# Five-layer transformer kernel on one core: setup reordered, keys and queries stored term by term, early keys and causal maxima moved

## The chip, the cores and the metric

The kernel runs on one core of a Trainium2 chip. The metric is the device time of one launch in microseconds (us). The engines are TensorE (PE, matmuls; PEld its weight loads), VectorE (DVE), ScalarE (ACT), GpSimd (POOL) and SyncE (SP). SP computes nothing here: it issues most DMAs. POOL issues weight loads.

## The reference, cut to what matters

Batch 1, 1024 tokens (x) of width 128, a context of 6404 tokens, 16 heads of width 8, everything in float32. There are four attentions. The first (cross0) attends from x to the context with a mask that drops up to a quarter of the context at its end; the second (self0) is plain self-attention; the third (self1) is causal; the fourth (cross1) attends to the same context without a mask. Each is followed by projections, layer norms or a feed-forward block.

```python
def _mha(q_in, k_in, v_in, Wq, Wk, Wv, bv, causal):
    q = jnp.einsum('bsd,hde->bhse', q_in, Wq)
    k = jnp.einsum('btd,hde->bhte', k_in, Wk)
    v = jnp.einsum('btd,hde->bhte', v_in, Wv) + bv[None, :, None, :]
    scores = jnp.einsum('bhse,bhte->bhst', q, k) * scale
    ...
    attn = jax.nn.softmax(scores, axis=-1)
    return jnp.einsum('bhst,bhte->bhse', attn, v)
...
x = x + _L0_xattn_ref(_layernorm(x), ctx_1024, mask, ...)   # cross0, masked
x = x + _L0_ffn_ref(_layernorm(x), ...)                     # self0, top-2 of 8 experts
x = x + _L1_xattn_ref(_layernorm(x), ctx_1024, ...)         # self1 causal, cross1, ffn
x = x + _L1_ffn_ref(_layernorm(x), ...)                     # top-2 of 8 experts, shared expert
```

## The kernel before, in words

**Precision by terms.** Scores must be accurate in float32, but the score matmuls run in bfloat16. So a projected key or query value is split into three bfloat16 parts (`split`): part 1 is the rounded value, the rest after it gives part 2, the rest after that part 3. A score is the sum of six products of parts, and the six stand below each other in the contraction: a head of width 8 takes 6 x 8 = 48 rows of a stage tile. `Q_PARTS` and `K_PARTS` (L38, L39) say which part stands in which of the six terms. Three further rows hold minus the query's maximum, also in three parts, and in cross0 one more row holds the mask.

**The split** works in jobs of 512 columns: PE projects into PSUM, ACT rounds to part 1 (L937), DVE subtracts (`take_rest`, L1104), ACT rounds to part 2 (L942), POOL subtracts to part 3 (L753), and SP stores the parts to DRAM (`store_parts`, L503): one DMA for the three parts of a key job (L511), six for a query job (L515), one for each term. There are four buffers of parts (`SPLITS`). cross0 has 13 key jobs and 2 query jobs, self0 and self1 two of each, cross1 has 2 query jobs. In cross0, before the split, DVE multiplies each projected key by `keep`, which is 1 or 0 by the mask (`make_keep`, L1173), from a mask that was loaded to all 128 partitions.

**Setup of cross0.** x is normalised and turned first, then the context is turned tile by tile (`turn_context`, L1835), projected and split. After the last key job SP writes the mask row and the row of ones into the four slots of both sides (`load_mask_row`, L491: 24 DMAs), then stores the query jobs.

**Staging.** A head is staged from DRAM into one of four slots of `k_stages` and `q_stages`, on two sides of 64 partitions: in a cross attention each side holds half of the keys (`stage_keys`, L522: three DMAs per side, of 24, 16 and 8 rows) and the same queries (`stage_queries`, L534); in a self attention each side is a head of a pair (`stage`, L594: the same three, and one for the queries).

**Main loops.** A cross attention makes 32 passes (16 heads, two halves of the queries). In each, 28 units of scores on PE (`pass_a`, L1677) go to DVE, which takes their maxima (L1234); maxima are joined, split by POOL (`split_maxima`), turned by PE, copied by ACT (`copy_turned`) and put into the query stage by SP (`put_maxima`, L546); then the scores are made again with the maximum subtracted (`pass_b`, L1719), ACT takes the exponential (L1028), and PE multiplies by the values. `pass_a` runs 40 units ahead (`a.ahead`). Between the first 28 units PE also projects the values of the context, 13 banks, which ACT copies out (L952). The 13 key jobs of cross1 (`early_jobs`) are done inside cross0, one in each of 13 of its second 16 passes, as one more item among the units (L1680 to L1690): DVE copies it (`take_key`), POOL alone splits it (`split_early`, L838).

**Self attentions** make 16 passes (8 pairs, two halves). `exps`, `evacuate` (ACT copies the sums out of PSUM in step 2 of the next pass, L969) and `store_out` (SP stores them, L616, and the next `evacuate` waits for that) follow the same pattern. The order on SP within a pass j is written out at L638 to L650:

```python
                for j in range(a.n):
                    pair, half = a.passes[j]
                    if half == 0 and pair >= 1 and pair + a.ring - 1 < H // 2:
                        sp.wait_ge(sem(a.name + "_scores"),
                                   pair_tile_use(a, j - 1, len(a.steps[j - 1]) - 1, a.sides - 1) + 1)
                        stage(pair + a.ring - 1)
                    if j + 1 < a.n:
                        put_maxima(j + 1)
                    if 1 <= j < a.n - 1:
                        store_out(j - 1)
```

In self1 the turn of the maxima of pass j + 1 comes in step 0 of pass j where j is even (`turn_step`), elsewhere in step 3. All order between engines is by semaphores, written by hand.

## Time and profile before

| | |
|---|---|
| median of 3 runs | 2730.98 us (2729.42 to 2733.01) |
| the profiled execution: its own time, its span | 2728.58 us, 2726.7 us |
| TensorE clock granted, mean over the span | 0.941 of full speed |
| busy: PE, DVE, ACT, POOL | 87%, 86%, 78%, 10% |
| cross0, until its first pass of exponentials runs | 0 to 141.7 us |
| cross0, main loop | 141.7 us to about 1114 us |
| self0 and its experts | to about 1394 us |
| self1 | to about 1590 us |
| cross1 and what follows | to the end |

The busy shares are means over stages with different limits. The chain of waits tells, at each moment, which work the end of the kernel hangs on; the timeline of a stretch tells what lies beside it.

### The profile page before, as it was taken

The page shows a single profiled execution, that of the slowest core. Times are in us where ns is not written, and L with a number is a line of the kernel's source. Part 1 is how long each engine was busy: PE and PEld are TensorE (multiplying, and loading weights), DVE is VectorE, ACT ScalarE, POOL GpSimd, SP SyncE. Part 2 cuts the span into 40 slices and gives each one's busy share as a digit, 9 for nine tenths or more (in the row PEclk, how much of TensorE's full clock was granted, in tenths as well). Part 3 has the DMA queues.
Part 4 walks back from the last instruction along what each step waited for, and adds up shares of the span by engine and source line. Part 5 has one row for each costly group of instructions (what it writes and reads, how often), then busy time and mean ns, then how long its engine had stood idle before and what let it go on. Part 6 is the DMA issues. An engine that isn't in the chain of part 4 may idle for free.

```text
span 2726.7 us, 59202 instructions
## 1 busy us (share of the span) xinstructions
PE 2384.8 (87%) x23163; PEld 751.8 (28%) x23163; DVE 2352.2 (86%) x2668; ACT 2134.0 (78%) x4065; POOL 274.8 (10%) x740
## 2 busy tenths in 40 slices
PE   4499999999999999489758848999999999999986
PEld 2222222222222222122322213222222222222224
DVE  6699999999999997499636649999999999999945
ACT  3189999999889899469615625999999999999971
POOL 5000110012111110100001100000000100000000
PEclk8799999999999999789878968999999999999998
DMA  4201111111111110111121030111111111111000
GB/s 144 73 24 41 41 35 45 43 44 41 47 49 41 41 43 7 46 50 33 36 61 41 30 99 4 38 34 30 30 40 33 30 30 41 31 30 32 17 3 8
DMA packets 75513, 107.98 MB, mean 40 GB/s; under 512 B 17061, under 2 KB 55849, under 8 KB 75241
## 3 DMA queue, kind: packets, MB, share of 16 engines
q1 hardware_dynamic: 73128, 99.79, 12.4%
q0 software_dynamic: 2112, 4.42, 0.9%
q8 instruction: 189, 3.10, 0.5%
q14 instruction: 84, 0.68, 0.1%
HBM read 73.45 MB, written 21.90 MB: 35 GB/s over the span
## 4 chain that ended last, share of the span: by engine, by line
PE 68%; DVE 18%; ACT 5%; SPq 3%; issue 3%; DMA 2%; POOL 0%; ACTq 0%; DVEq 0%
PE ps L1498 68%; DVE maxima L1234 12%; ACT probs L1028 4%; SPq L515 1%; DVE maxima L1193 1%; SPq L600 1%; ACT probs L986 1%; DVE scratch L1104 1%; DMA o_self<-acc_out 0%; PE ps L1504 0%; DVE stats L1110 0%; DMA scratch<-o_self 0%; DMA q_stages<-max_rows 0%; DVE z L1104 0%; DMA q_stages<-q_cross 0%
## 5 line engine op out<-in xcount | busy, mean ns | idle before, releaser
L1234 DVE TENSOR_REDUCE maxima<-ps 128x1 f32<-128x920 f32 x1792 | 1887.8, 1111 | 96.4 <-PE ps L1498 96.3
L1028 ACT ACTIVATE probs<-ps 128x512 f32<-128x512 f32 (+1 forms) x3264 | 1761.3, 594 | 159.9 <-PE ps L1498 159.7
L1498 PE MATMUL ps<-probs,v_stage 128*16 128x256 f32 x14208 | 1159.5, 393 | 0.6 <-ACT acc_out L1017 0.4
L1498 PE MATMUL ps<-k_stages,q_stages 64*128 64x460 bf16 (+2 forms) x4032 | 756.3, 373 | 187.3 <-DMA q_stages<-q_cross 64.4
L1498 PE MATMUL ps<-q_stages,k_stages 64*128 64x512 bf16 (+1 forms) x3712 | 725.8, 381 | 45.1 <-ACT probs L986 16.9
L1498 PEld LDWEIGHTS ps<-k_stages,q_stages 64*128 64x128 bf16 x4032 | 193.6, 93 | 1049.7 <-issue 494.3
L1498 PEld LDWEIGHTS ps<-probs,v_stage 128*16 128x16 f32 x14208 | 236.9, 94 | 412.2 <-issue 362.9
L1193 DVE TENSOR_REDUCE maxima<-ps 128x2 f32<-128x1024 f32 (+1 forms) x224 | 240.1, 1108 | 94.5 <-PE ps L1498 90.9
L986 ACT ACTIVATE probs<-ps 128x512 f32<-128x512 f32 x448 | 224.2, 554 | 72.7 <-PE ps L1498 71.7
L1498 PEld LDWEIGHTS ps<-q_stages,k_stages 64*128 64x128 bf16 x3712 | 187.4, 93 | 277.4 <-ACT probs L1028 69.4
L952 ACT ACTIVATE by_key<-ps 128x512 f32<-128x512 f32 (+1 forms) x30 | 17.5, 583 | 146.2 <-PE ps L1498 146.2
L759 POOL COPY v_stage<-by_key 128x400 f32<-128x400 f32 x64 | 33.1, 517 | 901.1 <-PE ps L1498 785.8
L811 POOL CAST half_parts<-neg_max 128x4 bf16<-128x4 f32 x64 | 11.9, 187 | 851.4 <-DVE neg_max L1253 794.5
L1104 DVE TENSOR_TENSOR scratch<-scratch 112x512 f32<-112x512 f32 (+1 forms) x14 | 13.6, 982 | 66.0 <-DMA scratch<-acc_out 39.7
L904 ACT ACTIVATE std<-var_eps 128x4 f32<-128x4 f32 x18 | 3.7, 205 | 70.9 <-DVE var_eps L1116 70.9
L1104 DVE TENSOR_TENSOR probs<-ps,probs 128x512 f32<-128x512 f32 x36 | 24.5, 689 | 19.8 <-ACT probs L1088 8.2
L1017 ACT ACTIVATE acc_out<-ps 128x512 f32<-128x512 f32 x64 | 38.2, 597 | 0.3 <-PE ps L1498 0.3
L1504 PE MATMUL ps<-ident,z 128*128 128x128 f32 x32 | 8.1, 403 | 32.0 <-DVE z L1126 18.5
L1504 PE MATMUL ps<-ident,xn 128*128 128x128 f32 x24 | 6.6, 430 | 31.5 <-DVE xn L1104 18.0
L783 POOL CAST max_parts<-neg_max 128x8 bf16<-128x8 f32 x32 | 6.1, 189 | 208.5 <-DVE neg_max L1204 162.4
L753 POOL TENSOR_TENSOR probs<-probs 128x512 bf16<-128x512 f32 x10 | 11.2, 1151 | 149.8 <-ACT probs L942 149.8
L1104 DVE TENSOR_TENSOR z<-ps,z 128x512 f32<-128x512 f32 (+2 forms) x10 | 6.7, 674 | 21.0 <-PE ps L1498 14.6
(233 smaller groups left out, 965.4 us busy)
## 6 DMA issues: line engine op xcount, KB each, us to landing
q_stages<-q_cross SPq DMA_DIRECT2D x256, 48.0 KB, 2.6
k_stages<-k_cross SPq DMA_DIRECT2D x64, 150.2 KB
k_stages<-k_cross SPq DMA_DIRECT2D x64, 150.0 KB
scratch<-acc_out SPq DMA_DIRECT2D x496, 16.0 KB
k_stages<-k_cross SPq DMA_DIRECT2D x64, 100.1 KB
k_stages<-k_cross SPq DMA_DIRECT2D x64, 100.0 KB
q_stages<-q_self SPq DMA_DIRECT2D x32, 192.0 KB
k_cross<-probs SPq DMA_DIRECT2D x12, 384.0 KB, 2.8
```

Of the source, the lines that this page charges most:

```text
L515: sp.dma_start(a.q_dram[:, term * E:(term + 1) * E, c0:c0 + n], src[:, part, 0:n]).then_inc(done, DMA)
L600: sp.dma_start(k_stage(a, slot)[base + row:base + row + parts_ * E, :], a.k_dram[0:parts_, h * E:(h + 1) * E, :]).then_inc(done, DMA)
L759: nc.gpsimd.tensor_copy(v_stage[:, par, 0:full, 0:E], src[:, 0:full, :]).then_inc(sem(a.name + "_v_staged"), 1)
L952: last = nc.scalar.activation(by_key[:, t:t + full, :], src[:, 0:full, :], ACT.Copy)
L986: return nc.scalar.activation(probs[:, i % a.p_slots, low:BANK], ps[:, b_bank(a, use), low:BANK], ACT.Exp, scale=float(E) ** -0.5)
L1017: nc.scalar.activation(acc_out[:], ps[:, ACC_BANK, :], ACT.Copy).then_inc(sem(a.name + "_acc_copied"), 1)
L1028: return nc.scalar.activation(probs[0:m, probs_slot(a, j, i), :], ps[0:m, b_bank(a, use), :], ACT.Exp, scale=float(E) ** -0.5)
L1104: return nc.vector.tensor_tensor(out_, a, b, op)
L1193: nc.vector.tensor_reduce(pair_maxima[:, j % 2, :, qt % QT, c // BANK], ps[:, A_BANK + 2 * (g % 2):A_BANK + 2 * (g % 2) + 2, 0:n], AX_X, A ...
L1234: nc.vector.tensor_reduce(maxima[:, at, seg:seg + 1], ps[:, A_BANK + 2 * (k % 2):A_BANK + 2 * (k % 2) + 2, 0:a.segment], AX_XY, ALU.max).t ...
L1498: return nc.tensor.matmul(out_, lhsT, rhs, start=start, stop=stop)
L1504: last = nc.tensor.transpose(ps[:, bank, t * P:(t + 1) * P], src[:, b * QT + t, :], ident[:])
```

## The change

1. **Setup order.** SP loads the weights and the first context tiles before x; the turning of x is moved from ahead of the context into jobs 4 and 6 (`SETUP_TURNS`). The constants that are not needed at once are made on POOL later, after the first maxima (`later_constants`).
2. **Mask.** Keys are no longer multiplied by `keep`; the mask row alone drops them. The mask is loaded to one partition. The row of ones is written early by 2 DMAs, the mask row by 2, where there were 24.
3. **Terms in DRAM.** DRAM now holds six terms of keys and of queries. A job of either kind is stored by three DMAs of 3, 2 and 1 terms (`store_job`), so a key job moves 768 KB where it moved 384 KB. Staging takes one DMA per side for keys and one for each query stage. The last job of each attention is stored from ACT's queue.
4. **Staging of self attentions** begins when all but the last query job is stored; pair 0 gets its first half of queries then and the remainder afterwards (`stage_rest`, awaited by `q_rest`).
5. **Early keys** of cross1 move out of the 13 passes to the first 28 units of cross0, where PE now has a value bank or an early key job after nearly every unit (`a.fill`). Here ACT copies and rounds, POOL makes both subtractions, SP stores; before its first exponential ACT waits until all are stored.
6. **Causal maxima.** In self1, on SP, `put_maxima(j + 1)` goes ahead of `stage` where `turn_step[j]` is 0.

```diff
-            sp.dma_start(x[:], x_dram).then_inc(sem("x_in"), DMA)
...
+                if t == 0:
+                    sp.dma_start(x[:], x_dram).then_inc(sem("x_in"), DMA)
...
+        def store_job(queue, a, i):
+            kind, c0, n = a.jobs[i]
+            src, done = a.parts[:, i % SPLITS, :, 0:n], stored(a, i)
+            queue.wait_ge(sem("split_part3"), a.jobs_before + i + 1)
+            first = 0
+            for part, terms in enumerate((3, 2, 1)):
+                if kind == "k":
+                    dst, part_ = a.k_dram, src[:, 0:terms]
+                else:
+                    dst, part_ = a.q_dram, src[:, part:part + 1].to_broadcast([P, terms, n])
+                queue.dma_start(dst[first:first + terms, :, c0:c0 + n].rearrange("a p c -> p a c"),
+                                part_).then_inc(done, DMA)
+                first += terms
...
-                    for row, parts_ in ((0, 3), (3 * E, 2), (5 * E, 1)):
-                        sp.dma_start(dst[base + row:base + row + parts_ * E, 0:count],
-                                     a.k_dram[0:parts_, h * E:(h + 1) * E, first:first + count]).then_inc(done, DMA)
+                    sp.dma_start(dst[base:base + ROW_MAX, 0:count],
+                                 a.k_dram[:, h * E:(h + 1) * E, first:first + count]).then_inc(done, DMA)
...
-                put_maxima(0)
+                if a is cross0:
+                    for i in range(len(early.jobs)):
+                        if i == len(early.jobs) - 2:
+                            put_maxima(0)
+                        store_job(sp, early, i)
+                else:
+                    put_maxima(0)
...
                 for j in range(a.n):
                     pair, half = a.passes[j]
+                    if a.turn_step[j] == 0 and j + 1 < a.n:
+                        put_maxima(j + 1)
                     if half == 0 and pair >= 1 and pair + a.ring - 1 < H // 2:
...
-                    if j + 1 < a.n:
+                    if a.turn_step[j] != 0 and j + 1 < a.n:
                         put_maxima(j + 1)
...
+                if a is cross0:
+                    wait_stored(act, early, len(early.jobs) - SPLITS, len(early.jobs))
...
-                        tt(a.whole[:, i % SPLITS, 0:n], ps[:, a.job_banks[i], 0:n], keep[:, c0:c0 + n],
-                           ALU.mult).then_inc(sem(a.name + "_whole"), 1)
...
-            for b in range(HALVES):
-                turn(b, xn, 1, 6 + b)
-            for b in range(HALVES):
-                half_turned(b, 1)
...
+                if i in SETUP_TURNS:
+                    b = SETUP_TURNS.index(i)
+                    if b == 1:
+                        half_turned(0, 1)
+                    turn(b, xn, 1, 3)
```

The order of the instructions, at three places. **SP, setup of cross0, before**, from the last key job to the first head (`k_cross` and `q_cross` are the DRAM copies, `probs` holds the parts):

```order
L511 DMA k_cross<-probs 128x3x260
L498 DMA k_stages<-k_stages 1x12x267
L501 DMA q_stages<-ones_row 1x16x64 x2
...
L515 DMA q_cross<-probs 16x8x512 x12
L529 DMA k_stages<-k_cross 24x1x3204
L529 DMA k_stages<-k_cross 16x1x3204
L529 DMA k_stages<-k_cross 8x3204
L529 DMA k_stages<-k_cross 24x1x3200
```

The same place now:

```order
L497 DMA k_cross<-probs 128x3x260
L497 DMA k_cross<-probs 128x2x260
L497 DMA k_cross<-probs 128x260
L538 DMA k_stages<-probs 1x4x3204
L538 DMA k_stages<-probs 1x4x3200
L497 DMA q_cross<-probs 128x3x512
L497 DMA q_cross<-probs 128x2x512
L497 DMA q_cross<-probs 128x512
L548 DMA k_stages<-k_cross 48x1x3204
L548 DMA k_stages<-k_cross 48x1x3200
L563 DMA q_stages<-q_cross 48x1x512 x2
```

Between the last key job and the first key DMA of a head there were 36 DMAs and are 5.

**PE, the first units of cross0, before** (460-column matmuls are two to a unit, 128-column ones are a value bank):

```order
L1498 MATMUL ps<-xT,w_q_cross 128x512 x2
L1498 MATMUL ps<-k_stages,q_stages 128x460 x6
L1498 MATMUL ps<-w_kv_cross,ctxT 128x128 x4
L1498 MATMUL ps<-k_stages,q_stages 128x460 x4
L1498 MATMUL ps<-w_kv_cross,ctxT 128x128 x4
L1498 MATMUL ps<-k_stages,q_stages 128x460 x4
```

Now (`w_k_cross` are early key jobs):

```order
L1559 MATMUL ps<-xT,w_q_cross 128x512 x2
L1559 MATMUL ps<-k_stages,q_stages 128x460 x4
L1559 MATMUL ps<-ctxT,w_k_cross 128x512
L1559 MATMUL ps<-k_stages,q_stages 128x460 x2
L1559 MATMUL ps<-w_kv_cross,ctxT 128x128 x4
L1559 MATMUL ps<-k_stages,q_stages 128x460 x2
L1559 MATMUL ps<-ctxT,w_k_cross 128x512
L1559 MATMUL ps<-k_stages,q_stages 128x460 x2
```

There is now a job between any two units, an early key job and a value bank by turns.

**SP, pass 2 of self1 now** (the first pass with staging; the passes 4, 6 and 8 read alike):

```order
L646 DMA q_stages<-max_rows 3x4x128 [waits self1_max_rows]
L646 DMA q_stages<-max_rows 3x4x128
L618 DMA k_stages<-k_self 48x1x1024 [waits self1_scores]
L626 DMA q_stages<-q_self 48x1x1024 x2
L618 DMA k_stages<-k_self 48x1x1024
L626 DMA q_stages<-q_self 48x1x1024 x2
L658 DMA o_self<-acc_out 2x8x512 [waits self1_acc_copied]
L658 DMA o_self<-acc_out 2x8x512 x3
```

Before, the two rows of maxima stood between the staging and the stores of `acc_out`, and the staging had 8 DMAs where it has 6.

## Rows read from the trace of the kernel before

**Rows 1.** The page: PE busy by fortieths, and the chain of waits by engine

```profile
PE   4499999999999999489758848999999999999986
...
PE 68%; DVE 18%; ACT 5%; SPq 3%; issue 3%; DMA 2%; POOL 0%; ACTq 0%; DVEq 0%
```

**Rows 2.** Windows of the setup (window, PE, PEld, DVE, ACT, POOL, clock, DMA share, GB/s)

```profile
60.00:80.00 20.00, 0.00 (x0) 0.00 (x0) 0.00 (x0) 0.00 (x0) 0.00 (x0) 0.50 0.29 76
...
100.00:120.00 20.00, 16.70 (x114) 10.65 (x113) 19.93 (x21) 5.79 (x10) 0.00 (x0) 1.00 0.20 69
```

**Rows 3.** Timeline of the setup (start, us, engine, line, operation; idle before it)

```profile
13.37 1.13 DVE L1126 TENSOR_SCALAR xn<-x,mean_var,rstd 128x128 f32<-128x128 f32 x4
...
21.83 0.63 ACT L937 ACTIVATE probs<-scratch 128x512 bf16<-128x512 f32 x1 [1.84 <-DVE scratch L1104]
...
29.27 26.49 SPq L511 DMA_DIRECT2D k_cross<-probs  x13
...
71.57 7.70 SPq L515 DMA_DIRECT2D q_cross<-probs  x12
81.21 3.88 SPq L529 DMA_DIRECT2D k_stages<-k_cross  x6
...
93.45 0.95 PE L1498 MATMUL ps<-k_stages,q_stages 64*128 64x460 bf16 x4 [41.45 <-DMA q_stages<-q_cross]
```

**Rows 4.** DMA view, 29 to 42 us, in 40 slices

```profile
GB/s 0 0 0 98 353 347 350 63 195 353 340 312 10 25 0 0 296 350 343 221 0 0 0 50 347 350 343 120 0 0 0 148 350 347 334 32 0 0 0 249
```

**Rows 5.** Timeline and chain of the first units of cross0

```profile
37.56 1.13 PE L1498 MATMUL ps<-ctxT,w_kv_cross 128*128 128x512 f32 x2 [0.94 <-ACT ctxT L917]
...
52.07 3.30 POOL L753 TENSOR_TENSOR probs<-scratch,probs 128x512 bf16<-128x512 f32 x3 [1.28 <-ACT probs L942]
...
112.25 1.16 PE L1498 MATMUL ps<-w_kv_cross,ctxT 128*128 128x128 f32 x8
```

**Rows 6.** Chain of waits over the whole span (start, us, what)

```profile
125.28 16.38 DVE maxima L1234 x16
...
595.81 17.82 PE ps L1498 x195
...
625.92 18.88 PE ps L1498 x197
...
1030.58 17.82 PE ps L1498 x195
```

**Rows 7.** Timeline around the staging of self0

```profile
1140.16 0.39 SPq L511 DMA_DIRECT2D k_self<-probs  x1
...
1151.78 1.94 SPq L600 DMA_DIRECT2D k_stages<-k_self  x3
...
1159.26 0.61 PE L1498 MATMUL ps<-k_stages,q_stages 64*128 64x512 bf16 x2 [19.58 <-DMA q_stages<-q_self]
```

**Rows 8.** Timeline of pass 2 of self1, and PE's waits from 1440 to 1584 us

```profile
1458.29 1.87 SPq L600 DMA_DIRECT2D k_stages<-k_self  x3
...
1460.50 0.26 ACT L966 ACTIVATE max_rows<-ps 24x128 bf16<-24x128 bf16 x1
...
1464.40 2.50 SPq L624 DMA_DIRECT2D o_self<-acc_out  x4
...
1466.06 0.39 PE L1498 MATMUL ps<-q_stages,k_stages 64*128 64x512 bf16 x2 [1.51 <-DMA q_stages<-max_rows]
...
1468.94 0.60 ACT L976 ACTIVATE acc_out<-ps 128x512 f32<-128x512 f32 x1
...
PE ps L1498 <- DMA q_stages<-max_rows: 8.9, 5, 2.2
```

**Rows 9.** Timeline around the staging of cross1, and the DMA rate from 1610 us

```profile
1610.33 13.11 SPq L515 DMA_DIRECT2D q_cross<-probs  x12
...
1630.86 0.95 PE L1498 MATMUL ps<-k_stages,q_stages 64*128 64x460 bf16 x4 [22.94 <-DMA q_stages<-q_cross]
...
GB/s 51 51 51 203 205 221 260 227 215 174 64 51 51 51 51 80 240 64 64 195 137 51 107 225 139 219 250 233 207 162 47 47 47 49 47 35 8 0 0 98
```

More of the change, by code:

```diff
@@ L235, in transformer @@
         SIDE = P // 2
-        ROWS_IN = cross0.sides * cross0.ring * 3
+        ROWS_IN = cross0.sides * 2
         QT = NT // HALVES
@@ L447, in moe1_banks, with q_rest_count @@
             return (5, 6, 7) if u % 2 == 0 else (0, 1, 2)
+        def q_rest_count(a):
+            return (1 + (a is self1)) * 2 * a.sides * DMA
         def b_bank(a, use):
@@ L459, in max_goal, with wait_stored @@
             return min(a.n * n, a.ahead + j * n + t + 1 + sum(t >= at for at in a.more_at))
+        JOB_DMAS = 3
         def stored(a, i):
+            if a is not early and i == len(a.jobs) - 1:
+                return sem("q1_stored")
             return sem(a.name + f"_stored{i % SPLITS}" if a.masked else a.name + "_stored")
         def stored_count(a, i):
-            jobs = range(i % SPLITS, i + 1, SPLITS) if a.masked else range(len(a.jobs))
-            return DMA * sum(TERMS if a.jobs[j][0] == "q" else 1 for j in jobs)
+            if a is not early and i == len(a.jobs) - 1:
+                return (attentions.index(a) + 1) * JOB_DMAS * DMA
+            return (i // SPLITS + 1 if a.masked else len(a.jobs) - 1) * JOB_DMAS * DMA
+        def wait_stored(queue, a, first, last):
+            for i in range(first, last):
+                queue.wait_ge(stored(a, i), stored_count(a, i))
+        def store_job(queue, a, i):
[11 more added lines that the diff above has]
+                first += terms
         RESULTS = ["cross0", "self0", "moe0", "self1", "cross1", "ffn", "moe1"]
@@ L671, in _ @@
                     sp.wait_ge(sem("self1_scores"), 2 * len(self1.all_steps) + self1.n)
-                    sp.wait_ge(sem("early_stored"), cross1.n_k_jobs * DMA)
+                    wait_stored(sp, early, len(early.jobs) - SPLITS, len(early.jobs))
                     for j in range(cross1.ring):
@@ L732, in _ @@
-            for late in (late_out["self0"], late_out["self1"]):
-                for g in range(4):
-                    col = late[:, g // 2, :] if late.shape[2] == VCOLS else late[:, g // 2, D:D + 1]
-                    first = 32 * g + (0 if late.shape[2] == VCOLS else E)
-                    link(nc.gpsimd.affine_select(out=col, in_=col, compare_op=ALU.not_equal, fill=1.0, base=-first,
-                                                 pattern=[[-1, col.shape[1]]], channel_multiplier=1))
             nc.gpsimd.memset(ones_row[:], 1.0)
@@ L958, in short_attention, with fill @@
+            def fill(a):
+                for kind, i in itertools.chain(*a.fill):
+                    if kind == "values":
+                        take_values(a, i)
+                    else:
+                        take_early(i)
+                if a is cross0:
+                    early_part2(len(early.jobs) - 1)
             def short_attention(a):
```

425 lines of the change are left out of this document (226 added, 199 removed).

## The prediction

> **What bounds the kernel now.** I read the page first. PE is the last link of the chain for 68% of the span, and the fortieths show it at nine tenths in two long stretches, the main loops of the cross attentions [rows 1]. The change hardly touches these; it works on the low digits between them. So I read the chain of waits over the whole span for where the loops begin and how long a pass takes, and the timeline of each gap for who releases whom.
>
> In the setup no engine computes from 60 to 80 us [rows 2]. The parts of the 13 key jobs are stored by 55.8 us (29.27 + 26.49); the query stores begin at 71.57 us. Between lie 24 small DMAs of mask and ones, 15.8 us in which SP alone is the limit. Then the query stores, their landing, the first staging at 81.21 us, and PE's first unit at 93.45 us, after 41.45 us idle [rows 3]. The main loop follows after 28 units (125.28 us) and 16 more units on DVE, at 141.7 us [rows 6]. A pass takes 30.1 us, but the 13 passes with an early key take 404.66 us together (625.92 to 1030.58), 31.13 each [rows 6]. The gaps at self0, self1 and cross1 look alike: PE idle for 19.6 and 22.9 us until a query stage lands [rows 7, 9]. In self1 PE waited 8.9 us for maxima, in five waits [rows 8].
>
> **The change part by part.** The sum is against the profiled execution, 2728.58 us.
>
> *First unit of cross0, from 93.45 to about 55.5 us: -38.* (a) Part 1 of job 0 was made at 21.83 us, behind the turning of x and the mask product [rows 3]. Now the context is turned while DVE normalises; DVE is free at 14.5 us (13.37 + 1.13), so I put part 1 at 15 us and the first store, which came 7.4 us behind part 1 and has less before it now (a subtraction and the product are gone), 4 us behind: 19 us. (b) Jobs came every 2.2 us in the mean, 12 periods from 29.27 to about 55.4 us. Now ACT has three copies of about 0.6 us per job, 1.8 us. But a key job stores 768 KB, and the store rate stands at 350 GB/s while a job is being written [rows 4]: 2.2 us. I take 2.2; 1.8, and 2.6 if DMA keeps only 300 GB/s, are the ends. 12.5 jobs and 2 us to land give 48.5 us (43 to 52). (c) The key DMAs of head 0 go then, 1.5 us of issue, but its queries wait for query job 0, which shares the DMA engines with job 1 on ACT's queue: 3 us more; then two query DMAs and their landing, some 4 us. That is 7 us from the first key DMA to the first unit; as now it would be 12.2 us (81.21 to 93.45) [rows 3], the upper end; with one third of the key DMAs 3.5 us is the lower. I take 7, nearer the lower, because the 12.2 is a queue: from 1625 us, while the last of it drains, the DMA moves 47 to 49 GB/s where 350 are possible, so few engines carry them [rows 4, 9], and six terms in one DMA should spread better than 3, 2 and 1. The Trainium skill (DMA: Bandwidth & Descriptors, "Why a DMA increments its semaphore by 16 and not by 1") says a DMA runs on the largest number of engines up to 16 that divides the outermost sizes of both its sides: 3 and 2 for the old key DMAs, 16 for the old query DMAs, 6 for both now. The tail of 50 GB/s agrees with that; by it the first unit would come about 5 us after the first key DMA and the sum would be 2 us lower. Loading x third instead of first costs nothing: DVE clears `k_stages` until 8.5 us anyway. The early weight is one DMA beside an 800 KB mask load that is gone. The constants made later on POOL cost nothing: about 15 us of POOL after the first maxima, while the next are needed 24 us on.
>
> *The first 28 units: +10.* They took 31.8 us (93.45 to 125.28), set by DVE at 1.02 us a unit behind a cold start. Now PE has 28 units of 0.27 us (0.95 us for two of them at half clock [rows 3], a little over half of that each at full), 13 value banks of 1.16 and 13 early jobs of 1.1 [rows 5]: 37 us at full clock. Part 3 on POOL takes 1.1 us [rows 5], two subtractions a job 2.3 us, and ACT's four copies about 2.3 us; both are below the 2.8 us that PE needs for a pair, so PE sets the pace. Before, the clock was full from 100 us, 7 us after PE began [rows 2]; in those 7 us an item takes twice as long, which costs 3 us: 40 us, +8. The first turn of maxima stands 4 units behind the 28th, and POOL reaches it only after the last early job, 7 to 8 us behind its projection: about 1.5 us late. ACT's wait for the last early stores (two puts of maxima, six stores, landing: 8 us behind the first maxima) ends when the first scores are ready, and so costs nothing; if stores run late it costs their lateness. Lower end +4 (DVE's pace with PE just behind), upper +28 (half clock throughout).
>
> *Main loop of cross0: -13.2*, that is 13 x 30.11 - 404.66 [rows 6].
>
> *self0: -2.5.* Staging began 11.6 us after the first store and the first unit came 7.5 us after that (1151.78 to 1159.26) [rows 7]. The stores are no faster: four jobs of 768 KB are 3.07 MB, 8.8 us at 350 GB/s [rows 4] and 2 to land, against 11.6. Pair 0 now needs four DMAs instead of eight, with half of the queries: 5 us. Ends 0 and -6. The remainder is needed a pass later and SP's total is 26 DMAs instead of 32, each dearer (below), so put_maxima(0) stays where it is.
>
> *self1: +6.5.* Its first unit gains the same 2.5 us, but SP's staging, not the unit, holds the first maxima, so 1 us is left. Then the four passes with staging. Before, maxima ready at 1460.76 waited for the staging (from 1458.29) and PE resumed at 1466.06. Now they go at once: PE could resume near 1464. But the staging, and behind it `store_out`, now stand behind that put. Ready 1460.76, the put 1.5, staging S, the stores 2.5 (1464.40 on) and 1.7 to land: 1466.5 + S. ACT's `evacuate` of this pass, which was at 1468.94, waits for that [rows 8]. S was 4.5 us for eight DMAs. A DMA whose two sides differ in shape, as the new six all do, took 0.6 to 0.7 us (1.87 us for the three key DMAs of a side) [rows 8], so S is about 4.3 and `evacuate` comes 1.9 us later: 4 x 1.9 = +7.5, less 1. If they cost 0.36 us like a plain store, S is 2.2 and nothing is lost; if the wait for maxima simply goes, -7. Ends -8 and +9.
>
> *cross1: -11.* Before, 12 query stores began at 1610.33 and PE at 1630.86, 20.5 us on, with 13.1 us of issue [rows 9]. Now query job 0 is three DMAs of SP's and job 1 three of ACT's: 1.54 MB, 4.4 us, 2 to land; then the query DMAs of head 0, 1.5 us and 2 to land: 9.5 us. Its keys are staged from 1587 us with 8 DMAs for 24 and are in before. Ends -9 and -13.
>
> Sum: -38 + 10 - 13.2 - 2.5 + 6.5 - 11 = -48. 2728.58 - 48 = 2680.6; the median of the runs is 2.4 us above the profiled execution, so **2683 us**. A measurement of this kernel tells 0.2%, 5.5 us, from no change.
>
> **The rivals.** *A, self1's waits vanish.* For it: 8.9 us of waits for maxima, four of the five in staging passes [rows 8]. Against: the stores' landing had no slack. If the six DMAs are cheap, self1 is -8 instead of +6.5: 2668 us. Chance 0.22.
>
> *B, the first units stay slow.* PE at half clock, or ACT waiting for early stores. For it: 0.50 of the clock stood from 60 to 80 us, and the early stores add 9.6 MB while three heads are staged. Against: PE has no idle there, and 9.6 MB is 28 us at 350 GB/s [rows 2, 4]. It takes back 15 to 25 us: 2703 us. Chance 0.12.
>
> *C, slower than before: a stage DMA of six terms runs on one engine.* If the tail's 50 GB/s are two engines, one moves 25 [rows 9]. A head is 792 KB of keys and queries; on one engine 31.7 us, above the 30.1 us of a pass [rows 6]. Both main loops would then be set by DMA: +1.6 x 62 passes = 99, the first unit +27, cross1's queries behind four heads of keys +60: 2683 + 186 = 2869 us. It decides once less than 792 KB / 30.1 us = 26 GB/s are reached. Against it: the tail alone still moves 47 to 49. Chance 0.03. The rule of the Trainium skill named above says six engines, so it speaks against C.
>
> *D, the early setup does not come off*: the jobs take 2.6 us and staging its 12.2 us; the first unit is at about 66 us: 2693 us. The chance, 0.08, is inside the range.
>
> **How the numbers follow.** The forecast has 0.55, A 0.22, B 0.12, D 0.08, C 0.03. The range takes A, D and most of B: 2662 to 2703 us. Faster by over 0.2% in all but C and an unknown mishap: 0.95; same 0.02; slower 0.03.
>
> **What the profile would show.** First unit of cross0 at 53 to 58 us; DMA near full from 19 to 46 us, and jobs every 2.2 us; 28 units in 38 to 43 us with PE over nine tenths; no pass of 31.1 us. self0 and self1: the first unit some 5 us behind the first staging DMA. In self1 SP's put of the maxima before the staging, ACT's `evacuate` behind a DMA, passes with staging 20 to 21 us a pair instead of 18.5 to 19.7. cross1: first unit 9 to 10 us behind the first store. Wrong I am if PE waits in the first units for ACT or the clock stays low there, if pairs in self1 take 17.5 us, or if any head of the main loops waits for its stage.

## The result, and the profile after

The changed kernel takes 2706.76 us (median of 4 runs, 2704.30 to 2708.58), the kernel before 2731.74 us (4 runs beside it). The ratio is 0.9909, with a 95% interval of 0.9892 to 0.9926: faster by 25 us, where the forecast was 48 us and its range ended at 2703. The sign was right and the size about half.

The page of the changed kernel, answering [rows 1]. Of the fortieths (68 us each) the second rose from 4 to 8, since the main loop begins sooner; but the 22nd and 23rd, which are self1, fell from 8 to 7. In the chain DVE fell from 18 to 15% and DMA rose from 2 to 4%.

```profile
PE   4899999999999999499757758999999999999986
...
PE 70%; DVE 15%; ACT 5%; DMA 4%; SPq 3%; issue 3%; POOL 1%; ACTq 0%; DVEq 0%; POOLq 0%
```

The profiled executions have spans of 2726.7 us before and 2702.6 us after, 24.1 us apart. Eight marks in both chains of waits show where the gain arose. Each mark is the start of the same piece of work; the gain so far is after minus before.

| mark | before | after | gain so far | this stage | forecast |
|---|---|---|---|---|---|
| first unit of cross0 | 93.45 | 65.44 | -28.0 | -28.0 | -38 |
| first PE piece of the main loop, behind 44 units | 141.71 | 129.56 | -12.2 | +15.8 | +10 |
| same piece, last pass but one | 1060.68 | 1035.12 | -25.6 | -13.4 | -13.2 |
| first unit of self0 | 1159.26 | 1129.76 | -29.5 | -3.9 | -2.5 |
| self1, PE's piece before the first staging pass | 1452.37 | 1420.46 | -31.9 | -2.4 | self1 in all: |
| self1, the same behind four staging passes | 1528.34 | 1515.16 | -13.2 | +18.7 | +6.5 |
| self1, load of the result | 1578.93 | 1567.56 | -11.4 | +1.8 | |
| main loop of cross1 | 1679.80 | 1655.56 | -24.2 | -12.9 | -11 |

The same rows of the chain of waits after the change (start, us, what), whole span cut at the stages:

```profile
58.02 7.29 DMA q_stages<-q_cross
...
77.34 7.97 DMA k_cross<-probs
...
129.56 1.53 PE ps L1559 x4
```

```profile
1420.46 7.14 PE ps L1559 x75
...
1436.99 4.48 DMA o_self<-acc_out
...
1443.51 8.72 PE ps L1559 x75
...
1461.60 4.18 DMA o_self<-acc_out
...
1515.16 9.98 PE ps L1559 x75
...
1567.56 5.01 DMA scratch<-o_self
```

So three stages missed, and they miss on the same side: the setup by 10 us, the first units by 6, self1 by 12 (18.1 in its three lines against 6.5). The main loop, self0 and cross1 came within 2 us of their terms.

**Setup.** The timeline of the setup, answering [rows 3] (start, us, engine, line, operation; idle before it):

```profile
14.04 0.60 ACT L988 ACTIVATE probs<-ps 128x512 bf16<-128x512 f32 x1 [1.16 <-PE ps L1559]
...
22.29 0.60 ACT L988 ACTIVATE probs<-ps 128x512 bf16<-128x512 f32 x1 [1.88 <-DMA k_cross<-probs]
...
49.61 0.60 ACT L988 ACTIVATE probs<-ps 128x512 bf16<-128x512 f32 x1 [1.82 <-DMA k_cross<-probs]
```

```profile
54.12 2.17 SPq L548 DMA_DIRECT2D k_stages<-k_cross  x2
57.29 1.42 SPq L563 DMA_DIRECT2D q_stages<-q_cross  x2
...
65.44 0.95 PE L1559 MATMUL ps<-k_stages,q_stages 64*128 64x460 bf16 x4 [20.97 <-DMA q_stages<-q_cross]
```

Part 1 of job 0 is made at 14.04 us and that of the fifteenth and last job at 49.61, so the jobs come every 2.54 us in the mean (35.57 / 14), not every 2.2. That mean holds the first four, which fill the four buffers 1.3 to 1.5 us apart. From the fifth on (22.29 us) ACT waits each time for the store of the job four before, and a job takes 2.73 us (27.32 / 10). The DMA engines are full meanwhile. The first key DMA goes at 54.12 us and not at 48.5, and PE's first unit follows 11.3 us later and not 7.

**First units.** Windows (window, PE, PEld, DVE, ACT, POOL, clock, DMA share, GB/s) and ACT's waits up to 130 us (engine, tile, line, releaser: us in total, times, longest), answering [rows 2]:

```profile
20.00:25.00 5.00, 4.15 (x20) 2.33 (x19) 2.95 (x5) 2.19 (x5) 1.84 (x2) 1.00 1.01 339
30.00:35.00 5.00, 1.77 (x7) 0.66 (x5) 3.14 (x5) 3.20 (x6) 1.71 (x2) 0.93 1.11 272
60.00:65.00 5.00, 0.00 (x0) 0.00 (x0) 0.00 (x0) 0.00 (x0) 0.00 (x0) 0.50 0.39 143
75.00:80.00 5.00, 5.00 (x29) 2.80 (x28) 3.98 (x5) 3.97 (x8) 4.05 (x5) 1.00 0.70 248
80.00:85.00 5.00, 2.63 (x14) 1.26 (x13) 3.27 (x3) 0.49 (x2) 1.84 (x2) 1.00 0.96 323
85.00:90.00 5.00, 3.94 (x11) 2.05 (x11) 1.12 (x1) 3.98 (x7) 2.76 (x3) 0.55 0.26 81
```

```profile
ACT probs L988 <- DMA k_cross<-probs: 15.7, 11, 2.3
...
ACT L1113 <- DMA k_cross<-probs: 8.0, 1, 8.0
ACT probs L1026 <- DMA k_cross<-probs: 7.9, 4, 4.9
```

PE is full at the full clock from 75 to 80 us, stops at 82.6 us, and goes on at 86.06 us at a clock of 0.55. ACT waited 4.92 us for the first early store, whose issue (76.38 us, on time) and landing (85.3 us) lie 8 to 9 us apart. Ahead of it in the queue were four heads of staging, four times 792 KB or 3.2 MB, which moved at 143 GB/s with a DMA share of 0.39. At the end ACT waits again, 8.0 us, for the last early stores, ahead of its first exponential.

**self1.** The waits of ACT from 1384 to 1584 us, and SP's timeline of the first staging pass, answering [rows 8]:

```profile
ACT acc_out L1060 <- DMA o_self<-acc_out: 23.3, 6, 6.2
```

```profile
1428.87 1.48 SPq L646 DMA_DIRECT2D q_stages<-max_rows  x2
1430.39 0.78 SPq L618 DMA_DIRECT2D k_stages<-k_self  x1
...
1434.97 2.60 SPq L658 DMA_DIRECT2D o_self<-acc_out  x4
```

```profile
1441.55 0.60 ACT L1060 ACTIVATE acc_out<-ps 128x512 f32<-128x512 f32 x1 [6.23 <-DMA o_self<-acc_out]
```

```profile
1442.69 0.61 PE L1559 MATMUL ps<-q_stages,k_stages 64*128 64x512 bf16 x2 [6.97 <-ACT probs L1070]
```

Before the change ACT's evacuation waited for DMA for 0.7 us in all of self1, now 23.3 us. The maxima go out at 1428.87, the staging from 1430.39 to 1434.97 (4.6 us), the stores behind it, and they land at 1441.5; ACT stands at its evacuation for 6.23 us and PE, which needs ACT's exponentials, for 6.97 us. Each such stop costs more than its own length: the granted clock, 1.00 before it, is 0.50 from 1442.5 to 1447 us, and PE's next piece of 75 matmuls takes 8.72 us (the line at 1443.51 above) where it took 7.14 us ahead of the stop.

### The profile page after: what moved, and what is told of

Its sections match the earlier page's. It is cut to its first block, busy times and chain, and to the rows that moved or that the text cites. A ratio compares the mean times of both kernels' runs of the same rounds, so it can differ in the third digit from the quotient of the medians.

```text
span 2702.6 us, 58908 instructions
## 1 busy us (share of the span) xinstructions
PE 2381.8 (88%) x23163; PEld 749.6 (28%) x23163; DVE 2334.1 (86%) x2629; ACT 2153.9 (80%) x4104; POOL 258.2 (10%) x720
## 4 chain that ended last, share of the span: by engine, by line
PE 70%; DVE 15%; ACT 5%; DMA 4%; SPq 3%; issue 3%; POOL 1%; ACTq 0%; DVEq 0%; POOLq 0%
PE ps L1559 69%; DVE maxima L1311 11%; ACT probs L1113 3%; DMA k_cross<-probs 1%; DMA o_self<-acc_out 1%; ACT probs L1070 1%; SPq L497 1%; SPq L626 1%; DVE maxima L1270 1%; SPq L658 1%; POOL probs L816 1%; SPq L618 0%; DVE stats L1202 0%; PE ps L1565 0%; DMA scratch<-o_self 0%
## 5 line engine op out<-in xcount | busy, mean ns | idle before, releaser
L1196 DVE TENSOR_TENSOR probs<-ps,probs 128x512 f32<-128x512 f32 x36 | 24.5, 688 | 19.7 <-ACT probs L1180 8.2
L1060 ACT ACTIVATE acc_out<-ps 128x512 f32<-128x512 f32 x32 | 19.2, 599 | 25.6 <-DMA o_self<-acc_out 23.3
L1102 ACT ACTIVATE acc_out<-ps 128x512 f32<-128x512 f32 x64 | 38.2, 597 | 0.2 <-PE ps L1559 0.2
L988 ACT ACTIVATE probs<-ps 128x512 bf16<-128x512 f32 (+1 forms) x25 | 14.7, 589 | 28.6 <-DMA k_cross<-probs 15.7
```

The costliest lines, as they stand in the source:

```text
L1102: nc.scalar.activation(acc_out[:], ps[:, ACC_BANK, :], ACT.Copy).then_inc(sem(a.name + "_acc_copied"), 1)
L1196: return nc.vector.tensor_tensor(out_, a, b, op)
```

## The experiments

The two theories I set against each other for what went missing: **backlog** (staging DMAs on few engines, issued ahead of urgent stores on the same queue, delay them), and **own cost** (the stores, the staging form or the landing cost what they cost wherever they stand). The ratios are all to the kernel before, which ran beside each batch: 2731.7 us beside the change, 2731.4 beside e1 to e4, 2729.4 beside f1 to f4 and 2730.3 beside g1 and g2. Differences of medians between batches, as in the last column, carry up to 2 us of that.

| run | median us | ratio, 95% interval | against the change |
|---|---|---|---|
| stores first in self1 (e1) | 2677.52 | 0.9808 (0.9791 to 0.9824) | -29.2 |
| old order in self1 (e2) | 2687.47 | 0.9842 (0.9826 to 0.9859) | -19.3 |
| heads 2 and 3 behind the early stores (e3) | 2704.12 | 0.9896 (0.9880 to 0.9913) | -2.6 |
| keys stored once (e4) | 2726.53 | 0.9979 (0.9970 to 0.9989) | +19.8 |
| e1 and first maxima of self1 early (f1) | 2674.98 | 0.9800 (0.9785 to 0.9815) | -31.8 |
| e1, e3 and maxima behind all early stores (f2) | 2669.61 | 0.9780 (0.9767 to 0.9793) | -37.2 |
| f1 and f2 together (f4) | 2667.96 | 0.9777 (0.9763 to 0.9790) | -38.8 |
| f4, and cross0's keys stored once (f3) | 2665.68 | 0.9765 (0.9752 to 0.9778) | -41.1 |
| rows layout alone (g1) | 2680.85 | 0.9824 (0.9810 to 0.9837) | -25.9 |
| f4 and rows layout (g2) | 2662.75 | 0.9757 (0.9744 to 0.9770) | -44.0 |

**e1: stores ahead of staging in self1.** Only the order of SP's instructions in that attention is changed:

```diff
                     if a.turn_step[j] == 0 and j + 1 < a.n:
                         put_maxima(j + 1)
-                    if half == 0 and pair >= 1 and pair + a.ring - 1 < H // 2:
+                    if not a.causal and half == 0 and pair >= 1 and pair + a.ring - 1 < H // 2:
                         ...
                         stage(pair + a.ring - 1)
                     if a.turn_step[j] != 0 and j + 1 < a.n:
                         put_maxima(j + 1)
                     if 1 <= j < a.n - 1:
                         store_out(j - 1)
+                    if a.causal and half == 0 and pair >= 1 and pair + a.ring - 1 < H // 2:
+                        ...
+                        stage(pair + a.ring - 1)
```

> Changed kernel, but in attention 1 of the second layer (self1) SP issues put of maxima, stores of the output, and only then the six staging DMAs. Theory (the stores stand behind 4.6 us of staging on SP, and then land in 4.5 instead of 2.5 us since the staging is ahead of them in the DMA queues, and ACT's evacuate waits for them): the four pairs of passes with staging take about 18.5 us instead of 24.3, the stores land in about 2.5 us, and the time falls by 20 to 24 us, to 2683-2687. Rival (the new staging DMAs themselves, six on few engines, hold up what PE and ACT need, wherever they stand): the pairs stay above 22 us and the time above 2698.

Measured 29.2 us less, more than the 20 to 24 expected. From the chain of waits of this run and ACT's waits in self1:

```profile
1421.35 7.14 PE ps L1564 x75
...
1433.82 2.50 DMA o_self<-acc_out
1438.29 7.23 PE ps L1564 x75
...
1489.24 7.22 PE ps L1564 x75
```

```profile
ACT acc_out L1065 <- DMA o_self<-acc_out: 1.1, 6, 0.2
```

A pair takes 17.0 us (67.9 for four) instead of 23.7 (94.7 for four), and the stores land in 2.50 us instead of 4.48. Another 2.9 us come in the passes behind (1489.24 to 1538.78, the load of the result, against 1515.16 to 1567.56). The staging DMAs are the same six with the same issue; only what stands behind them is different. The rival of own cost is out for self1. Part of the gain is clock: no stop, and the granted clock stays at 1.00 through the four pairs, so that PE's pieces of about 75 matmuls take 7.14 to 7.23 us where the changed kernel has 8.72, 8.53, 8.57 and, behind the fourth pair, 9.98 us; that is 4.4 us of the 26.8 in the pairs and nearly all of the 2.9 behind them. The kernel before also lost time here, 19.0 us a pair, but to another wait: PE waited 8.9 us in all for maxima that stood behind the staging.

**e2: the old order in self1** (staging, maxima, stores):

```diff
-                    if a.turn_step[j] == 0 and j + 1 < a.n:
-                        put_maxima(j + 1)
                     if half == 0 and pair >= 1 and pair + a.ring - 1 < H // 2:
                         ...
-                    if a.turn_step[j] != 0 and j + 1 < a.n:
+                    if j + 1 < a.n:
                         put_maxima(j + 1)
```

> Changed kernel with the order before in self1: staging, then maxima, then stores. Theory of the order: the pairs with staging take 19 to 20 us again as before the change, the time falls by 16 to 20 us, to 2687-2691. Rival (new form of the staging DMAs): nothing comes back, 2702 or more.

Measured 19.3 us less, as the theory of the order has it. Chain of waits of e2:

```profile
1423.62 5.89 PE ps L1557 x64
...
1500.07 7.14 PE ps L1557 x75
```

Four pairs take 76.4 us, against 76.0 before the change (1452.37 to 1528.34 in the table) and 94.7 in the changed kernel. So the one edit of putting the causal maxima ahead of the staging cost about 19 us by itself; the new form of the staging cost nothing measurable there. Of e1's 29 us, then, 19 undo this edit, and about 10 are gained on the old order.

**e3: heads 2 and 3 of cross0 staged behind the early stores.**

```diff
-                for j in range(a.ring):
+                for j in range(2 if a is cross0 else a.ring):
...
                     for i in range(len(early.jobs)):
                         ...
                         store_job(sp, early, i)
+                    for j in range(2, a.ring):
+                        stage_keys(a, j)
+                        stage_queries(j)
```

> Changed kernel, but in cross0 heads 2 and 3 are staged behind the stores of the early jobs instead of before them. Theory (the first early store waits 8 us for 3.2 MB of staging that moves at only 143 GB/s; PE then stops from 80.5 to 86 us and runs at half clock after it): the first early store lands in about 4 us, PE has no idle of over 2 us in the first 28 units, the main loop begins 7 to 9 us earlier, 2698-2700. Rival (the stores of early keys are limited by their own 786 KB a job): the stop only comes later, and under 3 us are won, 2704-2707.

In the profile the stop is gone. Windows and chain of e3:

```profile
70.00:80.00 10.00, 10.00 (x51) 5.62 (x51) 7.18 (x8) 6.93 (x14) 6.19 (x6) 0.93 0.23 82
80.00:90.00 10.00, 10.00 (x54) 5.27 (x54) 8.40 (x8) 8.21 (x15) 8.58 (x8) 1.00 0.87 297
```

```profile
65.74 20.64 PE ps L1562 x90
...
124.44 19.98 PE ps L1562 x195
```

PE is full from 70 to 90 us at a clock of 0.93 to 1.00, and the main loop begins at 124.44 instead of 129.56 us, 5.1 us sooner; expected were 7 to 9. The time fell by only 2.6 us, with intervals that overlap: by the times alone no gain is shown, and they lie where the rival had put them (2704 to 2707), while the trace shows the stop gone, as the theory had it. The chain of that run says where the gain went in one execution: PE's piece before the staging passes of self1 still is 3.8 us ahead (1416.64 against 1420.46), and behind the four staging passes 0.7 us (1514.47 against 1515.16), since they took 97.8 instead of 94.7 us. But the profiled execution of e3 is one of its slower ones (2706.36 of 2698.94 to 2707.53) and that of the changed kernel its fastest (2704.30), so that e3's own effect on self1 is not shown. In f2, where self1 is mended, the gain reaches the end.

**e4: key parts once in DRAM.** One store of 384 KB a key job of both cross attentions instead of three of 768 KB together; a head's keys staged by three DMAs a side:

```diff
-    a.stage_dmas = a.first_dmas = 2 * a.sides
+    a.stage_dmas = a.first_dmas = 4 * a.sides
...
-                    sp.dma_start(dst[base:base + ROW_MAX, 0:count],
-                                 a.k_dram[:, h * E:(h + 1) * E, first:first + count]).then_inc(done, DMA)
+                    for row, parts_ in ((0, 3), (3 * E, 2), (5 * E, 1)):
+                        sp.dma_start(dst[base + row:base + row + parts_ * E, 0:count],
+                                     a.k_dram[0:parts_, h * E:(h + 1) * E, first:first + count]).then_inc(done, DMA)
```

> Changed kernel, but key parts of both cross attentions lie once in DRAM (three terms, one store of 384 KB a job instead of three of 786 KB together), and a head's keys are staged by three DMAs a side as before the change. Theory (setup and early jobs are bound by the bytes stored, 786 KB at about 300 GB/s): jobs come every 1.9 to 2.1 us instead of 2.6, the last key part is stored 7 us earlier, and the slower staging takes back 3 to 5; first unit at 60 to 63 us instead of 65.4; ACT no longer stops for early stores except for the first; 2698-2703. Rival (jobs are bound by the chain ACT, DVE, ACT, POOL and the landing time of a store, not by bytes): jobs stay at 2.5 us or more, the first unit comes at 68 to 71 us, and the time is 2708 or more.

Slower than the change by 19.8 us. The time lies where the rival had it (2708 or more), but the rival's jobs of 2.5 us or more did not come, and the theory's time is missed by over 23 us. Part 1 of its jobs, its first unit, its windows and the largest pieces of its chain:

```profile
14.07 0.60 ACT L996 ACTIVATE probs<-ps 128x512 bf16<-128x512 f32 x1 [1.19 <-PE ps L1567]
...
40.05 0.60 ACT L996 ACTIVATE probs<-ps 128x512 bf16<-128x512 f32 x1 [0.58 <-DMA k_cross<-probs]
```

```profile
59.92 0.95 PE L1567 MATMUL ps<-k_stages,q_stages 64*128 64x460 bf16 x4 [21.31 <-DMA q_stages<-q_cross]
```

```profile
70.00:80.00 10.00, 6.89 (x40) 3.92 (x38) 6.70 (x6) 4.20 (x8) 5.15 (x5) 0.98 0.20 70
80.00:90.00 10.00, 0.00 (x0) 0.00 (x0) 0.00 (x0) 0.00 (x0) 0.00 (x0) 0.50 0.45 164
```

```profile
80.82 11.96 DMA k_cross<-probs
```

```profile
1609.30 16.23 DMA q_cross<-probs
```

With half of the bytes the jobs come every 1.86 us (14.07 to 40.05), and the first unit 5.5 us sooner. The edit also leaves one store DMA a job where there were three; but in the changed kernel the DMA engines are full and SP is not (39 stores of 0.53 us in 32 us), so it is the bytes stored that bind its setup. But with three DMAs a side the staging moves 70 GB/s at a DMA share of 0.20. SP gets its early stores out only at 80.82 us instead of 76.38, the first land 12 us behind their issue, PE waits 16.6 us from 77 us on, and the main loop begins 6.3 us later (135.89). At cross1 the query stores land in 16.2 us instead of 3.8, and its main loop begins 23.3 us later (1678.82). That is the backlog again, at half the rate. Neither expectation had priced it.

**f1: the first maxima of self1 ahead of the last pair's staging.**

```diff
                 for pair in range(a.ring):
+                    if a.causal and pair == a.ring - 1:
+                        put_maxima(0)
                     stage(pair)
...
-                put_maxima(0)
+                if not a.causal:
+                    put_maxima(0)
```

> The version with stores ahead of staging in self1, and there also the first put of maxima moved from behind all four pairs' staging to ahead of the last pair's. Theory (ACT has the maxima of pass 0 at 1398.7 us, SP gets to them at 1402.7, since it issues 26 staging DMAs of 0.74 us each first): 3 to 4 us less than the stores-first version, 2673-2675. Rival (something else holds pass 0, such as the landing of the staging): nothing, 2677-2678.

Measured 2.5 us less than e1, which ran in another batch, with ranges that overlap. The marks say that the edit itself brought less: from the end of the first key landing to the PE piece of the pass, 35.95 us (1386.92 to 1422.87) against 36.79 (1384.56 to 1421.35). SP's lateness was there, but DVE's maxima stood right behind it in the chain. The expectation of 3 to 4 us was a miss.

**f2: the order in cross0 as in e3, and the first maxima behind all early stores.**

```diff
                     for i in range(len(early.jobs)):
-                        if i == len(early.jobs) - 2:
-                            put_maxima(0)
                         store_job(sp, early, i)
+                    put_maxima(0)
```

> The version with stores ahead of staging in self1, and in cross0 heads 2 and 3 staged behind the early stores, and the first put of maxima behind all early stores instead of ahead of the last two jobs'. Theory (SP holds the last two jobs' stores back until the maxima are there, and ACT waits for their landing before its first exponential; heads 2 and 3 delay the first early store): the loop begins 5 us earlier by the staging as seen before and 3 to 4 more by the last stores, 2668-2671 in all, now that self1 can no longer eat it. Rival (the first scores need the maxima, and their put is what decides): only the 5 us, 2672-2673.

7.9 us less than e1, and the main loop starts at 123.24 instead of 130.27 us. Of these 7.0 us e3 alone had 5.1. The chain of f2 at this place:

```profile
105.59 10.24 DVE maxima L1318 x10
...
117.04 1.28 ACT L1120
...
123.24 16.81 PE ps L1566 x151
```

ACT's wait for the last early stores (8.0 us in the changed kernel, 9.1 in e3) is gone, but only 1.2 us came of it against e3 (123.24 for 124.44), where 3 to 4 were expected: DVE's maxima (16 units more) end only at 115.8 us. Even this is not told from chance: f4, whose code is the same up to here, has 121.79 us. The forecast's "costs nothing" for that wait was nearly right; what it cost is its excess over DVE.

**f3 and f4: the orders together, without and with keys stored once in cross0.** f4 is f1 and f2 together; f3 adds the edit of e4 for cross0 alone.

> The three changes of order together: stores ahead of staging and early first maxima in self1, heads 2 and 3 and the maxima behind the early stores in cross0. The terms stand in different stages and should add: 2677.5 - 3.5 - 5 - 3.5 = 2665 to 2667. If they do not (one eats another's gain, as self1 did), 2670 or more.

> All of these together, and cross0's keys stored once (three terms) and staged by three DMAs a side, cross1's as in the changed kernel. Theory (setup is bound by bytes stored; the price of that form was the staging at 70 GB/s of four heads ahead of the early stores and of cross1): first unit at 60 us instead of 65.4, early stores without the stop of 12 us, 5 us below the same version with six terms: 2661-2663. Rival (two heads staged at 70 GB/s still block the first early stores): PE stops at 80 us for 4 us or more, and the time is that of the other version or above, 2666 or more.

f4 took 2667.96 us, 1 us above what was expected. In f3 the first unit stands at 58.99 us and the main loop at 116.08 instead of 121.79 us; with two heads staged in front nothing blocks the early stores. Its median is 2.3 us below f4, with intervals that overlap, so of the 5.7 us of the mark less than half is shown in the time.

**g1 and g2: the same number of DMAs, with rows at one stride.** The layout in DRAM is [channel, term, key] instead of [term, channel, key]; the 48 rows of a head then lie at one stride, and nothing else is changed in g1:

```diff
-            a.k_dram = dram("k_" + a.name, [TERMS, P, a.keys], BF16)
+            a.k_dram = dram("k_" + a.name, [P * TERMS, a.keys], BF16)
...
-                queue.dma_start(dst[first:first + terms, :, c0:c0 + n].rearrange("a p c -> p a c"),
+                queue.dma_start(dst.rearrange("(p a) c -> p a c", a=TERMS)[:, first:first + terms, c0:c0 + n],
...
-                                 a.k_dram[:, h * E:(h + 1) * E, first:first + count]).then_inc(done, DMA)
+                                 a.k_dram[h * ROW_MAX:(h + 1) * ROW_MAX, first:first + count]).then_inc(done, DMA)
```

> Changed kernel with nothing moved; only the layout of keys and queries in DRAM is [channel, term, key] instead of [term, channel, key], so that a head's 48 rows lie at one stride and the two sides of a staging DMA have the same outermost size, 48. Theory (the changed kernel's staging DMAs run on 6 of 16 engines at about 143 GB/s and cost 0.74 us of issue because their sides differ in shape; what went wrong in fill and self1 is this backlog): issue falls to 0.35-0.4 us, staging runs at 250 GB/s or more, the first unit of cross0 comes 3 to 5 us sooner, PE's stop at 80 us goes (5 to 8 us), the self1 pairs with staging fall from 24.3 to about 19.5 us (18 to 20 us in all), self0 gains 1 to 2; together 28 to 34 us: 2673-2679. Rival (the landing and not the number of engines is what costs, or stores in this layout get slower): under 10 us, 2697 or more.

25.9 us less than the change, a little short of the 28 to 34. SP's timeline of a staging pass of self1, two windows of the staging in cross0, and the chain of g1:

```profile
1438.61 0.41 SPq L618 DMA_DIRECT2D k_stages<-k_self  x1
...
1441.40 2.52 SPq L658 DMA_DIRECT2D o_self<-acc_out  x4
```

```profile
63.00:66.00 3.00, 2.86 (x6) 0.66 (x6) 2.14 (x2) 0.00 (x0) 0.00 (x0) 0.50 1.00 165
66.00:69.00 3.00, 3.00 (x17) 1.56 (x16) 2.18 (x2) 1.84 (x4) 1.16 (x1) 0.95 1.08 206
```

```profile
1408.17 7.14 PE ps L1559 x75
...
1443.34 2.51 DMA o_self<-acc_out
...
1490.61 9.44 PE ps L1559 x73
```

The staging takes 2.8 us of issue instead of 4.6. Its heads in cross0 move at 165 to 206 GB/s with all DMA engines busy, instead of 143 with a share of 0.39; expected were 250 or more. The stores behind it land in 2.51 us, PE no longer stops at 80 us, and the main loop begins 6.7 us sooner (122.85). Another 5.6 us come by the start of self1's staging passes (1408.17 against 1420.46), from the stages between. Four pairs of self1 take 82.4 us, 12.3 less than in the changed kernel and 14.5 more than in e1, since the issue still stands ahead of the stores. The first unit came only 2.3 us sooner (63.14): the stores of query job 0, for which its queries wait, land at 57.50 us as before (57.27), and only the landing of the query DMA behind them is shorter, 5.14 us instead of 7.29.

> That layout together with the three changes of order. Theory: in self1 the order already removes what the backlog cost, so of the layout there remain the first unit of cross0 (3 to 5), self0, self1 and cross1 starts (1 to 2 each): 2668 - 6 to 10 = 2658-2662. Rival (the first unit is bound by the landing of a DMA whatever its engines): 2665 or more.

g2 has the lowest median of the study: 2662.75 us, ratio 0.9757 (0.9744 to 0.9770), 44 us below the changed kernel's; its interval overlaps those of f3 and f4. It is 5.2 us below f4, where 6 to 10 were expected. The marks put this between the main loop of cross0 and self1's staging passes (1285.9 us in g2, 1290.7 in f4); the main loop itself begins only 0.2 us sooner (121.57), and the first unit, at 64.44 us, gave not the 3 to 5 expected but 0.7.

## Why the prediction was wrong

**Setup, step (b), mis-sized: -28 instead of -38.** The mechanism was named rightly, a job's 768 KB set its pace, and the upper end of 2.6 us with 300 GB/s kept was in the text. I took 350 GB/s from [rows 4], a rate read while one 384 KB job was written at a time with gaps between. With stores back to back the windows show 339 GB/s of all traffic from 20 us, but 272 from 30 us, and once the buffers are full a job takes 2.73 us, which is 288 GB/s of stores (786 KB in decimal units), below even the 300 of the upper end. With the first four jobs the mean is 2.54 us; over the 12.5 periods of the sum that is 4.3 of the 5.6 us by which the first key DMA was late. The start was 1 us early (18.03 us for 19), and what is left, some 2 us, lies behind the last job: 4.5 us from its part 1 to the first key DMA, which SP issues behind the stores of query job 0. e4 shows the cause: half of the bytes, 1.86 us a job. At the first unit rival D came true, 65.4 us where it said about 66; the forecast of the whole had given it 0.08.

**Setup, step (c), mis-sized.** Between the first key DMA and the first unit lay 11.3 us, nearly the 12.2 of the kernel before, not 7. The 3 us until the queries may go were right (54.12 to 57.27 us, when the stores of query job 0 have landed); the "two query DMAs and their landing, some 4 us" took 8.2, of which the landing is 7.29. I argued that six terms spread better than 3, 2 and 1. They do: 143 GB/s, against 70 in e4. The share of 0.39 is six of sixteen DMA engines, and 143 GB/s is 24 for each, as the 47 to 49 of [rows 9] were for two. The Trainium skill (DMA: Bandwidth & Descriptors, "Why a DMA increments its semaphore by 16 and not by 1") says that such a DMA runs on 6 engines, the largest number up to 16 that divides both outer sizes; the trace agrees, and in g1, where the rule gives 16 for an outer size of 48, the share rose to 1.08. By the rule alone I had put the first unit 5 us behind the first key DMA, and that was wrong: it gives the number of engines, not what else stands in their queues. At 143 GB/s the keys of head 0, 600 KB, take 4.2 us, and the two query DMAs go out 3.2 us behind them. That accounts for a part of the 7.29 us only: from 57.0 to 65.4 us 1.22 MB moved, where keys and queries of head 0 are 0.70 MB together. 0.23 MB of it went over ACT's queue, on which query job 1 was being stored. No run puts the query DMAs ahead of the keys or takes job 1 away, so how the 7.29 us divide stays open.

**The first 28 units: +15.8 instead of +10.** "ACT's wait for early stores costs nothing; if stores run late it costs their lateness." They ran late, by 4.92 us at the first and less at three later ones, and behind PE's stop the granted clock was 0.50 from 86 to 92 us. This is rival B, at a third of its price. What I had not done is to add up what stands in the queue ahead of the first early store: four heads, 3.2 MB, issued from 54 to 74 us, at 143 GB/s 22 us. The prediction compared the 9.6 MB of early stores with 350 GB/s, but the staging cannot use that rate. e3 took out two heads and got 5.1 us back: from its first unit to its main loop it is 58.7 us (65.74 to 124.44), 10.4 more than before the change, where the forecast had +10. So the backlog accounts for this miss to within 1 us.

**self1: +18.1 instead of +6.5.** The formula had the right parts: SP's order is maxima, staging, stores, and ACT's evacuation waits for the landing. S was put at 4.3 us and is 4.6, four times 0.3. The landing was put at 1.7 us behind the last of the four issues, which is 2.3 us counted as the profile counts it, from the start of that issue; in e1 with nothing ahead it is 2.50, but behind six staging DMAs 4.48, 4.18, 3.90 and 3.22 us in the four passes, 6.6 us more than forecast in all. And the stops have a price that the formula left at nothing: PE at a granted clock of 0.50 behind each, 4.4 us over the pieces at 1443.51, 1467.82 and 1491.94 us. 7.5 + 1.2 + 6.6 + 4.4 is 19.7, and 18.7 were measured. So the terms that failed are "1.7 to land" and the clock behind the wait. Rival A, that the waits vanish, went the wrong way, and it had the largest chance of the rivals; the waits for maxima did shrink, from 8.9 to 1.5 us, but into a larger wait of ACT.

**Right:** the main loop of cross0 (-13.4 for -13.2), self0 (-3.9 for -2.5), cross1 (-12.9 for -11, first store 1598.16 us, PE 1606.35 us, 8.2 us where I had said 9.5). Rival C, one engine, did not happen. The range failed because its upper end took in one late stage (B), and here three were late together: the first units and self1 by the same backlog of staging, the setup by the rate of its stores. I had treated their errors as independent.

What stays open: how the 7.29 us of the first query landing divide between the keys ahead, the stores of query job 1 and what was issued behind, since no run changes them one by one, e4 and g1 moving several at once; and whether e3's staging passes of 97.8 us are chance or a result of its own order.

## What to carry to other kernels

Ahead of an order of DMA issues ask, for each store or put that an engine waits for, how many bytes stand before it in the same queue and at what rate these can move, and price its landing from that, not from a landing seen with an empty queue. Put what someone waits for first, and prefetches last: this cost nothing in code and was worth more (29 us, of which 19 undo one edit of the change) than the whole change. But a put that itself waits for data, as that of the maxima did, holds back all that SP would issue behind it. And a copy with few, wide DMAs is only as good as its outer dimensions: the same bytes in another DRAM layout moved 1.2 to 1.4 times as fast and cost SP 0.6 of the issue time.

## What the runs showed of the hardware

The issue of a staging DMA in self1 took 0.69 to 0.78 us on SP when the DRAM side was [6, 8, n] against 48 rows, and 0.42 us in the median (most 0.32 to 0.43, single ones up to 1.16) when it was 48 rows at one stride, for the same bytes. I had not expected what the rate did: with the first form 143 GB/s at a share of 0.39 of the DMA engines (window 60 to 65 us), with the second 165 to 206 GB/s at shares of 1.00 to 1.09 (g1, windows of 3 us from 63 to 75 us). Each engine moved about half as much, so more engines are not more bytes in proportion. Stores of 786 KB a job that followed each other without a gap kept 288 GB/s, where short bursts had shown 350. Four stores of 2.50 us of issue landed in 2.50 us (from the start of the last issue) with nothing ahead and in 3.22 to 4.48 us behind six staging DMAs; the first early stores behind 3.2 MB of staging in 8.0 us, and in e4, at the lower rate, in 12.0 us. The granted clock was 1.00 (2.4 GHz) from 75 to 82.5 us and 0.50 (1.2 GHz) from 86 to 92 us, behind a stop of PE of 3.4 us; in self1, behind stops of 5 to 7 us, it was 0.50 too (1442.5 to 1447 us).
